# Two convolutions on TensorE: weights first, side taps without the padding columns, and a new order of the lead-in work

## The chip, the cores and the metric

One core of one Trainium2 chip runs the kernel. The metric is the device time in microseconds (us) of one execution; smaller is better.

## The reference, cut to what matters

```python
# x: (16, 32, 128, 128) fp32; w3: (32, 32, 3, 3); w5: (32, 32, 5, 5)
w3 = w3 * mask            # mask per (input channel, tap): mean |w3| over outputs > threshold
x = x + conv3x3(groupnorm(x, 16 groups), w3, zero padding 1)
x = x + conv5x5(groupnorm(x, 16 groups), w5, zero padding 2) + bias
# the 5x5 one is written as an FFT product in the reference
```

## The kernel before, in words

Each image is cut into two halves of 64 rows, so there are HALVES = 32 half images and the main loop has STEPS = 35 steps. Step s does the 3x3 convolution of half s (for s below 32) and the 5x5 convolution of half s - 3 (LAG = 3). A half is held as four bands of 16 rows; band i lies on partitions 32i to 32i+31 with the 32 channels in them, plus halo rows. Rows are 128 pixels wide and lie at a pitch of 132, with two zero columns at each side.

To keep fp32 accuracy with fp16 matmuls, image and weights are each split into a high and a low fp16 part (x3_hi, x3_lo, x5_hi, x5_lo; s3_hi, s3_lo, s5_hi, s5_lo), and three products are summed in PSUM: high with high, image high with weight low, image low with weight high. A matmul contracts the 32 channels of one band and streams 4 rows of 128 pixels, 512 columns. `pairs` (L868) puts two vertical taps side by side, on tiles of 32x64, so that 8 matmuls of different bands and column halves run at the same time in the array; `singles` (L886) does the outer vertical taps, on 32x32 tiles, 16 at a time. I call these 8 or 16 simultaneous matmuls a group. Per step the 3x3 part has 18 pair groups and 9 single groups, the 5x5 part 60 and 15. In both functions the loop over the horizontal taps dx is outermost.

TensorE's order in a full step: `pairs3_high` (3x3, high image), `pairs3_low` (needs x3_lo), `pairs5_high` (needs x5_hi and a free PSUM half), `singles3`, `singles5`, `pairs5_low`, which ends the 5x5 sum (`b5_whole`). 

The other engines, in hand-written order, tied by semaphores:

- VectorE (DVE): `setup3` (mask and split of w3, starts at L592 when w3 and the threshold are in), `stats_in` (L615, mean and variance of the loaded bands, 4 instructions for a half), `combine` or `group_stats` and `scale_of` (the group norm's factors), `normalize3` (L691), `low3` (L719, makes x3_lo), `low5` (L727), `take_conv3` (L739, adds x to the 3x3 sum, making `mid`; it then frees the 3x3 banks with `bank3_go`), `stats_out` (L747), `aggregate` (L625, which tells ScalarE by `mv_ready`), and for the last steps `take_late` and `add_late` (L757, L764).
- ScalarE (ACT): `take_conv5` (L468, four instructions that empty the 5x5 banks into conv_out), then `x5_hi_go`, which lets `pairs5_high` start; `gather_stats` (a DMA that spreads every partition's statistics to all partitions), `take_root` (L385), `normalize5` (L438), `high3` (L392), `high5` (L431), and last in a step with an exchange `spread_stats`, which waits for `mv_ready` and sends the statistics to DRAM. ACT does these strictly in this order, so the `take_conv5` of the next step stands behind `spread_stats`.
- GpSimd (POOL): the zero rows, then the DMAs that move `mid` of half 1 into bands (L363), then `add_out` (L369), which adds conv_out to `mid`.
- SyncE (SP): the other DMAs: `load_bands`, `load_own` (x again, in the layout of the output), `move_mid`, `store_out`.

Statistics of x for a pair of halves are exchanged in steps 2 and 4 and then in odd steps (`exchanged`); the 5x5 statistics in odd steps from 3. From half LATE = 29 on, ACT takes only two of the four 5x5 banks and DVE the other two.

Of the kernel before, what the change touches and what calls it, by code (L numbers as in the profile page):

```python
# [30 lines left out]
C = 32  # L31
Q = 4
# [17 lines left out]
def two_blocks(nc, x, w3_dram, thr_dram, w5_dram, bias_dram, mix_dram, out):  # L50
# [7 lines left out]
    with ExitStack() as ctx:  # L58
# [66 lines left out]
        w5_bounded = sem("w5_bounded")  # L125
        w5_hi_made = sem("w5_hi_made")
# [72 lines left out]
        LATE = HALVES - LAG  # L199
# [47 lines left out]
        def _(sp):  # L247
# [35 lines left out]

            load_bands(0)
            load_bands(1)
            load_bands(2)
            for q in range(Q):
                sp.dma_start(w5[quad(q), :, :], w5_dram.rearrange("i a b o -> i (a b) o")).then_inc(w_loaded, 16)
                sp.dma_start(bias[quad(q), :], bias_dram.rearrange("(o a) -> o a", a=1)).then_inc(w_loaded, 16)
# [51 lines left out]
        def _(pool):  # L341
# [18 lines left out]
            for i in range(Q):  # L360
                for j in range(Q):
                    to, rows = piece(1, i, j)
                    pool.dma_start(to, rows).then_inc(mid1_moved, 16)  # L363

# [6 lines left out]
            for k in range(LAST):  # L371
                for b in range(BANKS if k < LATE else HALF_BANKS):
                    add_out(k, b)
                if k == LATE:
                    pool.wait_ge(norm2, HALVES)
                    m = mid[:, LAST % MID_SLOTS, :, :]
                    nc.gpsimd.tensor_scalar(m, m, bias[:, 0:1], None, ALU.add).then_inc(bias_added, 1)

        @block.scalar
        def _(act):  # L380
# [39 lines left out]
            def high_w5():  # L420

                act.wait_ge(w5_bounded, 1)
                nc.scalar.activation(s5_hi[:, :, :], w5[:, :, :], ACT.Identity,
                                     bias=zeros[:, 0:1], scale=wfac[:, 1:2]).then_inc(w5_hi_made, 1)
# [38 lines left out]
            def take_conv5(k, b):  # L463

                act.wait_ge(b5_whole, k + 1)
# [22 lines left out]
            act.dma_start(mix_in[:, :], mix_dram).then_inc(mix_loaded, 16)  # L488
            by_scalar = 1
# [5 lines left out]
            for s in range(STEPS + 1):  # L495
# [5 lines left out]
                if HALVES < s <= LAST + LAG:  # L501
                    act.wait_ge(late_out, s - HALVES)
# [38 lines left out]
        def _(dve):  # L541
# [207 lines left out]
            def take_late(k):  # L749

                dve.wait_ge(b5_whole, k + 1)
                if k == LATE:
                    dve.wait_ge(out_added, BANKS * LATE)
                else:
                    dve.wait_ge(late_added, k - LATE)
# [4 lines left out]
            def add_late(k):  # L760
# [8 lines left out]
            set_apart("x", 0)  # L769
            dve.drain().then_inc(bank3_go, 1)  # L770
# [15 lines left out]
            dve.wait_ge(w_loaded, 16 * 2 * Q)  # L786
            largest(w5, 1)
# [26 lines left out]
            for s in range(LAG + 1, STEPS):  # L814
                gathered = exchanged(s - 1)
                if s > HALVES:
                    take_late(s - 1 - LAG)
                low5(s - LAG)
                if s > HALVES:
                    add_late(s - 1 - LAG)  # L820
# [11 lines left out]
                if s % 2:  # L832
# [14 lines left out]
                if has3(s + 1):  # L847
                    low3(s + 1)
# [9 lines left out]
        def _(pe):  # L858
            def pairs(w, src, k, bank, start=False, every=None):

                for dx in range(k):
                    x0 = 2 - k // 2 + dx
                    for dy in range(1, k):
                        at = dx * k + k - 1 - dy
                        for i in range(Q):
                            for J in range(2):
                                top = 2 * J + dy
                                ins = nc.tensor.matmul(  # L868
                                    psum[2 * C * J:2 * C * (J + 1), bank + i, :].rearrange("p (a w) -> p a w", a=A),
                                    w[quad(i), at:at + 2, :].rearrange("p t o -> p (t o)"),  # L870
                                    src[quad(i), top:top + A * (A - 1) + 1:A, x0:x0 + W],
                                    start=start and dx == 0 and dy == 1, stop=True, skip_group_check=True,
# [5 lines left out]
            def singles(w, src, k, bank, start=False):  # L878

                for dx in range(k):  # L880
                    x0 = 2 - k // 2 + dx
                    for i in range(Q):
                        for j in range(Q):
# [3 lines left out]
                                psum[quad(j), bank + i, :].rearrange("p (a w) -> p a w", a=A), w[quad(i), at, :],  # L887
                                src[quad(i), j + dy:j + dy + A * (A - 1) + 1:A, x0:x0 + W],
                                start=start and dx == 0, stop=True, skip_group_check=True, tile_position=(i * C, j * C))
# [130 lines left out]
```

## Time and profile before

| | |
|---|---|
| median of 3 runs | 823.47 us (822.88 to 823.75) |
| the profiled execution | 823.28 us |
| its span, first to last instruction | 821.5 us |
| PE busy / DVE / ACT / POOL | 756.0 / 608.8 / 333.9 / 265.3 us |
| matmuls | 32292 |
| mean granted TensorE clock | 0.980 |
| DMA | 150.76 MB, mean 184 GB/s |

The span is 1.8 us shorter than the profiled execution, which is 0.2 us below the median of the runs. Engines overlap; PE is busy 92% of the span, so the question at each place is whether PE waits there, and for whom. L with a number is a line of the kernel; an engine's name with q (ACTq, DVEq) is its instruction queue.

### The profile page before, as it was taken

Reading aid. Unit: us, or ns where it says so; the run is one execution under the profiler, and the core shown is the slowest. Engines: PE = TensorE matmul, PEld = TensorE weight load, DVE = VectorE, ACT = ScalarE, POOL = GpSimd, SP = SyncE. Lnnn points to the kernel's source line nnn. Section 1 sums busy time; section 2 is a strip of 40 time slices with the busy share of each in tenths; the row PEclk is TensorE's granted clock in tenths of the full one; section 3 lists DMA queues with packets and bytes.
Section 4 is the critical chain, followed back from the end, with each engine's and each line's share of the span. In section 5 each row is a group of like instructions: output and inputs, shape, how many; then the busy total and the mean of one; then the engine's idle time right before and its main releaser. Section 6 shows DMA issues by size and latency. Waiting matters only on the chain.

```text
span 821.5 us, 67804 instructions
## 1 busy us (share of the span) xinstructions
PE 756.0 (92%) x32292; PEld 528.7 (64%) x32292; DVE 608.8 (74%) x970; ACT 333.9 (41%) x289; POOL 265.3 (32%) x161
## 2 busy tenths in 40 slices
PE   0585898899999999999999999999999999998996
PEld 0252484568767667767766766776776676676664
DVE  2888757797878969787879878787878786663341
ACT  0252314344443636344443536353443436362420
POOL 1021034044434332233434343222434343322360
PEclk9997898999999999999999999999999999999998
DMA  9879399989997989899897979898997956673424
GB/s 203 158 143 224 75 217 227 230 205 220 195 222 171 220 195 221 196 218 212 202 217 168 219 183 227 196 225 198 215 219 181 220 116 161 137 167 86 99 51 102
DMA packets 234400, 150.76 MB, mean 184 GB/s; under 512 B 18752, under 2 KB 227712, under 8 KB 230272
## 3 DMA queue, kind: packets, MB, share of 16 engines
q1 hardware_dynamic: 227200, 143.93, 80.8%
q10 hardware_dynamic: 6464, 5.24, 2.7%
q0 software_dynamic: 704, 1.25, 0.6%
q8 instruction: 10, 0.16, 0.1%
q14 instruction: 22, 0.18, 0.1%
HBM read 75.86 MB, written 33.59 MB: 133 GB/s over the span
## 4 chain that ended last, share of the span: by engine, by line
PE 82%; DVE 8%; DMA 4%; issue 2%; DVEq 1%; ACT 1%; ACTq 1%
PE psum L868 63%; PE psum L886 20%; DMA every_mv<-mv_scratch 2%; DVE bn_in L615 2%; DMA thr<-L_conv_threshold_dram 1%; DVE x_lo L719 1%; DVE bn_out L747 1%; DMA mv_scratch<-mv 1%; DVE mid L739 1%; DVEq L742 1%; ACT conv_out L468 0%; ACTq L506 0%; ACTq L486 0%; DVE x_bands L691 0%; ACT x_hi L399 0%
## 5 line engine op out<-in xcount | busy, mean ns | idle before, releaser
L369 POOL TENSOR_TENSOR mid<-mid,conv_out 128x512 f32<-128x512 f32 x120 | 246.0, 2082 | 484.0 <-ACT conv_out L468 484.0
L868 PE MATMUL psum<-x_hi,s_hi 32*64 32x512 f16 x6656 | 201.3, 384 | 18.2 <-ACTq L506 6.2
L868 PE MATMUL psum<-x_lo,s_hi 32*64 32x512 f16 x6656 | 200.1, 383 | 5.9 <-DVE x_lo L719 5.9
L868 PE MATMUL psum<-x_hi,s_lo 32*64 32x512 f16 x6656 | 199.7, 381 | 0.0
L868 PEld LDWEIGHTS psum<-x_hi,s_hi 32*64 32x64 f16 x6656 | 122.0, 105 | 85.9 <-issue 11.2
L868 PEld LDWEIGHTS psum<-x_hi,s_lo 32*64 32x64 f16 x6656 | 133.6, 105 | 53.6 <-issue 4.3
L868 PEld LDWEIGHTS psum<-x_lo,s_hi 32*64 32x64 f16 x6656 | 108.9, 104 | 83.8 <-issue 11.6
L739 DVE SCALAR_TENSOR_TENSOR mid<-psum,unscale,x_own 128x1024 f32<-128x1024 f32 x64 | 79.1, 1278 | 90.5 <-PE psum L886 90.4
L468 ACT ACTIVATE conv_out<-psum,bias,unscale 128x512 f32<-128x512 f32 x120 | 83.7, 777 | 69.7 <-PE psum L868 60.7
L392 ACT ACTIVATE x_hi<-x_bands 128x2304 f16<-128x2304 f32 x31 | 65.6, 2117 | 106.2 <-PE psum L886 106.2
L727 DVE TENSOR_TENSOR x_lo<-mid_bands,x_hi 128x2560 f16<-128x2560 f32 x32 | 93.8, 2932 | 6.9 <-PE psum L868 6.8
L431 ACT ACTIVATE x_hi<-mid_bands 128x2560 f16<-128x2560 f32 x31 | 72.5, 2339 | 50.8 <-PE psum L886 48.8
L385 ACT ACTIVATE root<-gvar 128x1 f32<-128x1 f32 x32 | 6.5, 203 | 207.7 <-DVE gvar L668 175.2
L438 ACT ACTIVATE mid_bands<-mid_bands,nbias,gscale 128x2560 f32<-128x2560 f32 x31 | 78.2, 2524 | 16.0 <-DVE nbias L682 13.6
L747 DVE BATCH_NORM_STATS2 bn_out<-mid 128x6 f32<-128x512 f32 x128 | 79.1, 680 | 4.1
L719 DVE TENSOR_TENSOR x_lo<-x_bands,x_hi 128x2304 f16<-128x2304 f32 x32 | 80.7, 2522 | 0.6 <-ACT x_hi L392 0.2
L615 DVE BATCH_NORM_STATS2 bn_in<-x_bands 128x6 f32<-128x512 f32 x128 | 76.7, 663 | 2.6 <-DMA x_bands<-x_dram 2.6
L886 PE MATMUL psum<-x_hi,s_hi 32*32 32x512 f16 x4096 | 74.3, 378 | 1.8 <-issue 1.7
L886 PE MATMUL psum<-x_hi,s_lo 32*32 32x512 f16 x4096 | 73.4, 376 | 0.0
L691 DVE TENSOR_SCALAR x_bands<-x_bands,gmean,gscale 128x2304 f32<-128x2304 f32 x29 | 67.8, 2339 | 0.5 <-ACT x_hi L403 0.4
L886 PE MATMUL psum<-x_lo,s_hi 32*32 32x512 f16 x4096 | 66.2, 377 | 1.4 <-issue 1.4
L886 PEld LDWEIGHTS psum<-x_hi,s_hi 32*32 32x32 f16 x4096 | 53.6, 88 | 19.7 <-issue 15.7
(91 smaller groups left out, 338.3 us busy)
## 6 DMA issues: line engine op xcount, KB each, us to landing
x_own<-x_dram SPq DMA_DIRECT2D x128, 256.0 KB, 5.0
mid_bands<-mid SPq DMA_DIRECT2D x372, 80.0 KB, 3.4
out_dram<-mid SPq DMA_DIRECT2D x116, 256.0 KB, 5.3
x_bands<-x_dram SPq DMA_DIRECT2D x96, 288.0 KB, 6.1
x_bands<-x_dram SPq DMA_DIRECT2D x32, 272.0 KB, 6.9
mid_bands<-mid SPq DMA_DIRECT2D x124, 64.0 KB, 2.9
every_mv<-mv_scratch ACTq DMA_DIRECT2D x17, 256.0 KB, 4.1
out_dram<-mid SPq DMA_DIRECT2D x20, 128.0 KB, 2.4
```

The costliest lines, as they stand in the source:

```text
L369: nc.gpsimd.tensor_tensor(m, m, conv_out[:, b, :], ALU.add).then_inc(out_added, 1)
L431: nc.scalar.activation(x5_hi[:, :, 2:2 + W], mid_bands[:, k % MB_SLOTS, :, :], ACT.Copy).then_inc(hi5_done, 1)
L438: nc.scalar.activation(v, v, ACT.Identity, bias=nbias[:, at], scale=gscale[:, at]).then_inc(act_scaled, 1)
L468: nc.scalar.activation(conv_out[:, b, :], psum[:, X5_BANK + b, :], ACT.Identity, bias=bias[:, 0:1], scale=unscale[:, 1:2]).then_inc(conv5_ ...
L615: nc.vector.bn_stats(bn_in[:, h // 2 % 2, h % 2, b, :], rows.rearrange("p a w -> p (a w)")).then_inc(bn_x, 1)
L691: nc.vector.tensor_scalar(v, v, gmean[:, 0:1], gscale[:, 0:1], ALU.subtract, ALU.mult).then_inc(scaled, 1)
L719: nc.vector.tensor_tensor(x3_lo[:, :, 2:2 + W], x_bands[:, h % XB_SLOTS, :, :], x3_hi[:, :, 2:2 + W], ALU.subtract).then_inc(x3_lo_go, 1)
L727: nc.vector.tensor_tensor(x5_lo[:, :, 2:2 + W], mid_bands[:, k % MB_SLOTS, :, :], x5_hi[:, :, 2:2 + W], ALU.subtract).then_inc(x5_lo_go, 1)
L739: nc.vector.scalar_tensor_tensor(mid[:, h % MID_SLOTS, at, :], psum[:, X3_BANK + at.start:X3_BANK + at.stop, :], unscale[:, 0:1], x_own[:, ...
L747: nc.vector.bn_stats(bn_out[:, h % 2, b, :], mid[:, h % MID_SLOTS, b, :]).then_inc(bn_mid, 1)
L868: ins = nc.tensor.matmul(psum[2 * C * J:2 * C * (J + 1), bank + i, :].rearrange("p (a w) -> p a w", a=A), w[quad(i), at:at + 2, :].rearran ...
L886: ins = nc.tensor.matmul(psum[quad(j), bank + i, :].rearrange("p (a w) -> p a w", a=A), w[quad(i), at, :], src[quad(i), j + dy:j + dy + A ...
```

## The change

Four things are changed.

1. Loads and weights. w3 is loaded first, half of it by SP ahead of the first bands and half by ACT; w5 is loaded before the bands of half 2; bias goes to ACT's queue, on a semaphore of its own. `largest(w5)` is done in the start by DVE, before `bank3_go`; POOL scales w5 and makes s5_lo; ACT's `high_w5` moves from step 1 to step 2 and waits for POOL's scaling.
2. LATE is 28 in place of 29, so one more half has its banks shared by ACT and DVE.
3. DVE's order. In step 4 (LAG + 1) `low3(5)` comes before the `stats_in` of halves 6 and 7. In step 5 (the only step where `just_now` holds) `take_conv3(5)` and `low3(6)` come before the `stats_in` of halves 8 and 9, and `stats_out(5)` after them.
4. Matmuls. The taps go in the order center, then outward; a tap at distance d from the center reads and writes 128 - d columns of each of its 4 rows (508 or 504 in place of 512), so the output in PSUM is 4 runs of 127 or 126 with gaps.

```diff
-        LATE = HALVES - LAG
+        LATE = HALVES - LAG - 1
...
+            for q in range(Q // 2):
+                sp.dma_start(w3[quad(q), :, :], ...).then_inc(w3_loaded, 16)
             load_bands(0)
             load_bands(1)
-            load_bands(2)
             for q in range(Q):
                 sp.dma_start(w5[quad(q), :, :], ...).then_inc(w_loaded, 16)
-                sp.dma_start(bias[quad(q), :], ...).then_inc(w_loaded, 16)
+            load_bands(2)
             load_bands(3)
...
                     pool.dma_start(to, rows).then_inc(mid1_moved, 16)
+            pool.wait_ge(w5_bounded, 1)
+            nc.gpsimd.tensor_scalar(w5[:, :, :], w5[:, :, :], wfac[:, 1:2], None, ALU.mult).then_inc(w5_scaled, 1)
+            pool.wait_ge(w5_hi_made, 1)
+            nc.gpsimd.tensor_tensor(s5_lo[:, :, :], w5[:, :, :], s5_hi[:, :, :], ALU.subtract).then_inc(w5_split, 1)
...
             def high_w5():
-                act.wait_ge(w5_bounded, 1)
-                nc.scalar.activation(s5_hi[:, :, :], w5[:, :, :], ACT.Identity,
-                                     bias=zeros[:, 0:1], scale=wfac[:, 1:2]).then_inc(w5_hi_made, 1)
+                act.wait_ge(w5_scaled, 1)
+                nc.scalar.activation(s5_hi[:, :, :], w5[:, :, :], ACT.Copy).then_inc(w5_hi_made, 1)
...
-            for q in range(Q):
+            for q in range(Q // 2, Q):
                 act.dma_start(w3[quad(q), :, :], ...).then_inc(w3_loaded, 16)
             act.dma_start(thr[:, :], ...).then_inc(w3_loaded, 16)
             act.dma_start(mix_in[:, :], mix_dram).then_inc(mix_loaded, 16)
+            for q in range(Q):
+                act.dma_start(bias[quad(q), :], ...).then_inc(bias_loaded, 16)
...
                     normalize3(3)
-                    high_w5()
                 elif s == 2:
                     high3(3)
+                    high_w5()
                     take_root(("mid", 0))
...
             stats_in(1, range(BANKS))
             set_apart("x", 0)
+            dve.wait_ge(w_loaded, 16 * Q)
+            largest(w5, 1)
             dve.drain().then_inc(bank3_go, 1)
...
             low3(2)
-            dve.wait_ge(w_loaded, 16 * 2 * Q)
-            largest(w5, 1)
             power_of_two(1)
...
             low3(LAG)
-            dve.wait_ge(w5_hi_made, 1)
-            nc.vector.scalar_tensor_tensor(s5_lo[:, :, :], w5[:, :, :], wfac[:, 1:2], s5_hi[:, :, :],
-                                           ALU.mult, ALU.subtract).then_inc(w5_split, 1)
...
-                if s % 2:
+                if s % 2 and not just_now:
                     for h in (s + 3, s + 4):
                         if has3(h):
                             stats_in(h, range(BANKS))
                 if has3(s):
                     take_conv3(s)
+                if just_now:
+                    low3(s + 1)
+                    for h in (s + 3, s + 4):
+                        stats_in(h, range(BANKS))
+                if has3(s):
                     stats_out(s)
                 if s == LAG + 1:
+                    low3(s + 1)
                     for h in (2 * LAG, 2 * LAG + 1):
                         stats_in(h, range(BANKS))
                     aggregate("x", LAG, mv_ready)
...
-                if has3(s + 1):
+                if has3(s + 1) and s != LAG + 1 and not just_now:
                     low3(s + 1)
...
+            def columns(k):
+                for dx in sorted(range(k), key=lambda d: abs(d - k // 2)):
+                    x0 = 2 - k // 2 + dx
+                    yield dx, x0, max(0, 2 - x0), min(W, W + 2 - x0)
...
-                for dx in range(k):
-                    x0 = 2 - k // 2 + dx
+                for dx, x0, c0, c1 in columns(k):
...
-                                    psum[...].rearrange("p (a w) -> p a w", a=A),
+                                    psum[...].rearrange("p (a w) -> p a w", a=A)[:, :, c0:c1],
...
-                                    src[quad(i), top:top + A * (A - 1) + 1:A, x0:x0 + W],
-                                    start=start and dx == 0 and dy == 1, stop=True, skip_group_check=True,
+                                    src[quad(i), top:top + A * (A - 1) + 1:A, x0 + c0:x0 + c1],
+                                    start=start and dx == k // 2 and dy == 1, stop=True, skip_group_check=True,
```

`singles` is changed in the same way. The conditions on `s > HALVES` around `take_late`, `add_late` and `late_out` follow LATE.

## Rows read from the trace of the kernel before

**Rows 1.** The page: busy time, and the groups of instructions with their mean

```profile
PE 756.0 (92%) x32292; PEld 528.7 (64%) x32292; DVE 608.8 (74%) x970; ACT 333.9 (41%) x289; POOL 265.3 (32%) x161
...
L719 DVE TENSOR_TENSOR x_lo<-x_bands,x_hi 128x2304 f16<-128x2304 f32 x32 | 80.7, 2522 | 0.6 <-ACT x_hi L392 0.2
```

**Rows 2.** The chain that ended last, in order of time: start, length, what

```profile
3.83 11.01 DMA thr<-L_conv_threshold_dram
...
22.52 4.77 DVE bn_in L615 x8
...
132.43 7.69 DMA mv_scratch<-mv
140.14 8.00 DMA every_mv<-mv_scratch
```

**Rows 3.** Windows: stretch, length, busy of PE, PEld, DVE, ACT, POOL, clock, DMA

```profile
208.70:231.50 22.80, 22.76 (x1008) 17.65 (x1000) 19.14 (x38) 10.49 (x10) 8.27 (x4) 1.00 0.93 209
```

**Rows 4.** Timeline of PE in one step: start, length, instruction, count

```profile
737.65 4.61 PE L868 MATMUL psum<-x_hi,s_hi 32*64 32x512 f16 x160
...
742.02 4.63 PE L868 MATMUL psum<-x_hi,s_lo 32*64 32x512 f16 x160
...
749.65 1.37 PE L886 MATMUL psum<-x_hi,s_hi 32*32 32x512 f16 x80
...
750.75 1.37 PE L886 MATMUL psum<-x_hi,s_lo 32*32 32x512 f16 x80
```

**Rows 5.** Timeline, the warming matmuls of L936, alone on PE

```profile
28.65 6.10 PE L936 MATMUL psum<-warm 128*128 128x512 f16 x14
...
51.67 1.90 PE L936 MATMUL psum<-warm 128*128 128x512 f16 x8
```

**Rows 6.** L868 at 737.64 to 738.51 (dx 0), then 738.51 to 739.39 (dx 1): min/median/max ns

```profile
L868 PE MATMUL psum<-x_hi,s_hi x32: 372/374/377, 737.6 to 738.4; 32*64 32x512 f16 x32
...
L868 PE MATMUL psum<-x_hi,s_hi x42: 372/377/381, 738.1 to 739.2; 32*64 32x512 f16 x42
```

**Rows 7.** The start: timeline of DVE, and issues at 0.7 to 1.2, 2.1 and 5.2 with us to landing

```profile
14.94 0.46 DVE L592 TENSOR_REDUCE score<-w 128x9 f32<-128x288 f32 x1 [13.13 <-DMA thr<-L_conv_threshold_dram]
...
w<-L_conv_weight_dram ACTq DMA_DIRECT2D x2, 36.0 KB, 5.4
...
w<-L_conv_weight_dram ACTq DMA_DIRECT2D x1, 36.0 KB, 7.8
...
x_bands<-x_dram SPq DMA_DIRECT2D x2, 272.0 KB, 11.0
```

**Rows 8.** Timeline around the weights of the 5x5 part, and POOL's bias instruction

```profile
55.71 9.21 POOL L363 DMA_DIRECT2D mid_bands<-mid  x16 [50.73 <-DVE mid L739]
...
60.44 1.05 ACT L423 ACTIVATE s_hi<-w,zeros,wfac 128x800 f16<-128x800 f32 x1 [2.53 <-DVEq L789]
...
67.46 0.20 ACT L385 ACTIVATE root<-gvar 128x1 f32<-128x1 f32 x1 [3.95 <-DVE gvar L653]
...
782.64 6.41 POOL L377 TENSOR_SCALAR mid<-mid,bias 128x2048 f32<-128x2048 f32 x1
```

**Rows 9.** Timeline of steps 4 to 6, with the waits that matter

```profile
132.86 2.79 ACT L468 ACTIVATE conv_out<-psum,bias,unscale 128x512 f32<-128x512 f32 x4 [3.02 <-DVE mv L625]
...
134.86 2.79 PE L868 MATMUL psum<-x_lo,s_hi 32*64 32x512 f16 x48 [3.64 <-DVE x_lo L719]
...
137.43 5.99 PE L868 MATMUL psum<-x_hi,s_hi 32*64 32x512 f16 x160
...
163.87 2.79 ACT L468 ACTIVATE conv_out<-psum,bias,unscale 128x512 f32<-128x512 f32 x4 [5.98 <-DVE mv L625]
...
167.22 4.59 PE L868 MATMUL psum<-x_hi,s_hi 32*64 32x512 f16 x160
```

**Rows 10.** Timeline of PE at the start of steps 32 and 33

```profile
759.61 4.61 PE L868 MATMUL psum<-x_hi,s_hi 32*64 32x512 f16 x160 [2.96 <-ACTq L506]
...
778.25 4.61 PE L868 MATMUL psum<-x_hi,s_hi 32*64 32x512 f16 x160 [1.61 <-ACTq L506]
```

More of the change, by code:

```diff
@@ L125, in two_blocks @@
         w5_bounded = sem("w5_bounded")
+        bias_loaded = sem("bias_loaded")
+        w5_scaled = sem("w5_scaled")
         w5_hi_made = sem("w5_hi_made")
@@ L282, in move_edges @@
                                      ).then_inc(mid_bands_in[2 * n % MB_SLOTS], 16)
+            for q in range(Q // 2):
+                sp.dma_start(w3[quad(q), :, :], w3_dram.rearrange("i a b o -> i (a b) o")).then_inc(w3_loaded, 16)
             load_bands(0)
             load_bands(1)
-            load_bands(2)
             for q in range(Q):
                 sp.dma_start(w5[quad(q), :, :], w5_dram.rearrange("i a b o -> i (a b) o")).then_inc(w_loaded, 16)
-                sp.dma_start(bias[quad(q), :], bias_dram.rearrange("(o a) -> o a", a=1)).then_inc(w_loaded, 16)
+            load_bands(2)
             load_bands(3)
@@ L373, in _ @@
                     add_out(k, b)
-                if k == LATE:
+                if k == LATE + 1:
+                    pool.wait_ge(bias_loaded, 16 * Q)
                     pool.wait_ge(norm2, HALVES)
@@ L463, in take_conv5 @@
             def take_conv5(k, b):
+                if k == 0 and b == 0:
+                    act.wait_ge(bias_loaded, 16 * Q)
                 act.wait_ge(b5_whole, k + 1)
@@ L488, in _ @@
             act.dma_start(mix_in[:, :], mix_dram).then_inc(mix_loaded, 16)
+            for q in range(Q):
+                act.dma_start(bias[quad(q), :], bias_dram.rearrange("(o a) -> o a", a=1)).then_inc(bias_loaded, 16)
             by_scalar = 1
@@ L500, in _ @@
                         take_conv5(k, b)
-                if HALVES < s <= LAST + LAG:
-                    act.wait_ge(late_out, s - HALVES)
+                if LATE + LAG < s <= LAST + LAG:
+                    act.wait_ge(late_out, s - LATE - LAG)
                 if s == LAG:
@@ L752, in take_late @@
                 if k == LATE:
+                    dve.wait_ge(bias_loaded, 16 * Q)
                     dve.wait_ge(out_added, BANKS * LATE)
@@ L815, in _ @@
                 gathered = exchanged(s - 1)
-                if s > HALVES:
+                if s > LATE + LAG:
                     take_late(s - 1 - LAG)
                 low5(s - LAG)
-                if s > HALVES:
+                if s > LATE + LAG:
                     add_late(s - 1 - LAG)
@@ L868, in pairs @@
                                 ins = nc.tensor.matmul(
-                                    psum[2 * C * J:2 * C * (J + 1), bank + i, :].rearrange("p (a w) -> p a w", a=A),
+                                    psum[2 * C * J:2 * C * (J + 1), bank + i, :].rearrange("p (a w) -> p a w", a=A)[:, :, c0:c1],
                                     w[quad(i), at:at + 2, :].rearrange("p t o -> p (t o)"),
-                                    src[quad(i), top:top + A * (A - 1) + 1:A, x0:x0 + W],
-                                    start=start and dx == 0 and dy == 1, stop=True, skip_group_check=True,
+                                    src[quad(i), top:top + A * (A - 1) + 1:A, x0 + c0:x0 + c1],
+                                    start=start and dx == k // 2 and dy == 1, stop=True, skip_group_check=True,
                                     tile_position=(i * C, 2 * C * J))
@@ L876, in pairs, with singles @@
                 return ins
-            def singles(w, src, k, bank, start=False):
-                for dx in range(k):
-                    x0 = 2 - k // 2 + dx
+            def singles(w, src, k, bank):
+                for dx, x0, c0, c1 in columns(k):
                     for i in range(Q):
@@ L886, in singles @@
                             ins = nc.tensor.matmul(
-                                psum[quad(j), bank + i, :].rearrange("p (a w) -> p a w", a=A), w[quad(i), at, :],
-                                src[quad(i), j + dy:j + dy + A * (A - 1) + 1:A, x0:x0 + W],
-                                start=start and dx == 0, stop=True, skip_group_check=True, tile_position=(i * C, j * C))
+                                psum[quad(j), bank + i, :].rearrange("p (a w) -> p a w", a=A)[:, :, c0:c1], w[quad(i), at, :],
+                                src[quad(i), j + dy:j + dy + A * (A - 1) + 1:A, x0 + c0:x0 + c1],
+                                start=False, stop=True, skip_group_check=True, tile_position=(i * C, j * C))
                 return ins
```

## The prediction

> **What bounds the kernel now.** I read the page first: PE is busy 756 of 821.5 us [rows 1]. The chain of waits then shows where it is not the bound: the start, which waits for a DMA of the threshold, and the lead-in up to 167 us, where DVE and two exchanges through DRAM hold the chain [rows 2]. The windows show that from 186 us on every full step takes 22.80 us with PE busy all the time at the full clock (one such step stands in [rows 3]); this repeats up to 756 us. So TensorE's own pace sets the middle, DVE and DMA the lead-in, and short waits for ACT the last steps [rows 10]. The DMA engines are at 0.93 in the step shown, which leaves room for a step shorter by one per cent.
>
> Next, what sets PE's pace. The 160 pair matmuls of one product take 742.02 - 737.65 = 4.37 us, for 20 groups of 8, so 219 ns a group; 80 singles take 750.75 - 749.65 = 1.10 us, 220 ns for a group of 16 [rows 4]. A warming matmul alone, with the same 512 columns, goes at (1.90 - 0.39)/7 = 0.216 us at the full clock and at 6.10/14 = 0.43 us at the lower one (2.4 and 1.2 GHz) [rows 5]. A group of 8 or of 16 thus costs what one stream of 512 columns costs, 213 ns at 2.4 GHz, and some 6 ns. Columns are what is paid for, not instructions. Of the 6 ns a part comes from where the read starts: the matmuls of tap 0 have a median of 374 ns, those of tap 1, which start at an odd column, 377 [rows 6].
>
> **The change part by part.** *Columns.* A side tap at distance 1 streams 4 columns fewer, 1.67 ns, and one at distance 2 streams 8 fewer, 3.33 ns. Per step the 3x3 part has 27 groups, 18 of them at distance 1: 30 ns. The 5x5 part has 75, of which 30 at each distance: 150 ns. Together 0.18 us of 22.80, 0.8%. Where PE is the bound (5x5 of halves 2 to 31 and 3x3 of halves 6 to 31) that is 30 x 0.150 + 26 x 0.030 = 5.3 us, and about 0.2 more before that: **-5.5 us**. What the trace doesn't show is a matmul that writes runs with gaps: all of them write 512 columns in one piece. Bounds: on the side of a gain, the start column costs 3 ns at most [rows 6] and the new starts (2, 2, 2, 3, 4 in place of 0 to 4) could give that back at one tap in five, another 0.05 us a step or 1.5 us; on the other side, the nearest row of a slower stream is the lower clock, twice the time, taken up among the rivals. I take the column count.
>
> The Trainium skill ("PSUM — Partial Sum Buffer", specifications, and "Advanced Engine Details and Errata", PSUM Cachelines) speaks against this: PSUM has 8-byte lines, and an access pattern in which not every two consecutive elements are contiguous slows matmuls significantly. No run here shows it so far; by it the term would be a loss, which the first rival works out from rows.
>
> *Start.* DVE's first work waits 13.13 us for the threshold, which was issued at 3.83 and took 11.0 us, behind four loads of w3 on its queue and in competition with twelve loads of bands [rows 2, 7]. Now only two w3 loads are ahead of it on that queue, and it is issued at about 1.7. Late bound: the first two w3 loads took 5.4 us in the median (the second was in at about 7.1), and the threshold follows as long after them as it followed the last one before (3.83 + 11.01 = 14.8, less 2.1 + 7.8 = 9.9: 4.9 us), at 12.0: a gain of 2.9 us. Early bound: it takes 5.4 us like those loads and lands at 7.1: 7.8 us. From there on the bands of half 1 bind as well: they landed at 16.4 at the latest (issued at 5.2 to 5.7, 11.0 us) [rows 7] and come 0.9 us later now, and their statistics started at 24.9 [rows 2]. Since the bands no longer run ahead of the weights I take a value on the early side, a landing at 8.1: **-6.8 us**. All that follows in the start hangs on this: statistics, their mixing on PE, factors, first matmul. The added `largest` (0.98 us) covers most of the 0.77 us that DVE waited for that mixing: **+0.3**. The wait for w5 costs nothing: with w3 (0.15 MB), two halves (2.3) and itself (0.4) it has 2.9 MB to wait for, 14 us at the 209 GB/s of [rows 3] and some 2 to start, and DVE gets there at about 21. Nor do the own rows of half 0, 6.2 MB in all and in at about 32, hold up DVE's first take of a 3x3 sum.
>
> *w5 on POOL.* ACT's `high_w5` now stands behind POOL, whose 16 DMA issues run until 55.71 + 9.21 = 64.92 [rows 8], 9.2 us after the second half's `mid` whatever DVE does (times as before, the start's shift left out). Scaling 800 elements at 6.41/2048 = 3.1 ns each takes 2.5 us: 67.4. The copy takes ACT about 1.0 [rows 8], until 68.5. Queued behind it on ACT is `take_root` of the first 5x5 statistics, which ran at 67.46. Behind that are `scale_of`, `low3(3)` and `high5_first`, and PE waits for both. DVE itself loses two instructions of 1.0 us, but they are not late any more, the root is: **+1.1 us** (0.9 to 1.8 if POOL is slower while DVE runs). s5_lo is ready at about 71.8, before x5_hi at 72.9.
>
> *DVE's order in steps 4 and 5.* PE waited 3.64 us for x3_lo of half 5 [rows 9], and `low3(5)` comes first now. But ACT's take of the 5x5 banks waited for `mv_ready` (3.02 us) and so did the next one (5.98 us) [rows 9], since `spread_stats` stands ahead of it, and x5_hi_go behind. In step 4 `low3` (2.5 us [rows 1]) now stands ahead of the aggregate: mv_ready at 134.9 in place of 132.4 [rows 2], conv_out (2.79 us) until 138.3, and the 5x5 pairs start at 138.4 where they started at 137.43. PE only waits in another place. The exchange, two DMAs of 7.7 and 8.0 us [rows 2], starts 2.5 us later, and what hangs on it in step 5 too. There `low3(6)` again stands ahead of the aggregate, another 2.5 us. So mv_ready of step 5 comes 5 us later, and the 5x5 pairs, which started at 167.22 half a us after x5_hi_go, start **4.7 us** later; ahead of that PE has only the 3x3 pairs to do (4 us) and idles for some 8. Bounds: if the DMAs, which compete with bands and moves, land when they landed before, 2.3; no gain is possible here, since the chain between the aggregates only gets longer.
>
> *The clock.* After the idle stretch before 134.86 the clock was at the lower level, and 48 + 160 matmuls took 2.79 + 5.99 us where full speed takes 1.53 + 4.6 [rows 4, 9]: 2.6 lost. Before, PE came out of this place at 167 at full speed. Now it comes out of a longer idle stretch: **+2.4**, 0 to 3.
>
> *LATE.* In step 32 PE waited 2.96 us for ACT's four banks, in step 33, where DVE takes two, 1.61 [rows 10]. Step 32 now goes like 33: **-1.4**. DVE's added 3.6 us there have the 9 us of pairs [rows 4] as cover; without it they would come back in full.
>
> Sum: -6.8 + 0.3 + 1.1 + 4.7 + 2.4 - 1.4 - 5.5 = -5.2. The profiled execution took 823.28 (span 821.5 and 1.8 around it), which gives 818.1; the median of the runs is 0.2 above it: **818.3 us**, 0.6% faster.
>
> **The rivals.**
>
> *Runs of 127 are written slowly.* Suppose that writes go well only by pairs of neighbouring columns: an odd run then puts half of its rows out of step, and each pair there is written twice. Two of four rows at half pace, which is that of the lower clock [rows 5], add 2 x 127/2.4 = 106 ns to each group at distance 1. There are 48 of them a step, so 5.1 us, and the kernel would take about 823 + 30 x 5 = 970 us. It decides from little: 78 side groups a step share 5.2 + 5.5 = 10.7 us of advantage, 0.36 us a step, so 4.6 ns more per side group than I assume makes the kernel slower. For it: nothing in the trace shows a gapped write. Against it: odd starts and rows at a pitch of 132 on the reading side cost 3 ns a group, not 100 [rows 6]. Chance 0.15. This is what the rule of the Trainium skill's PSUM page, named above, would do here.
>
> *The columns save nothing.* A run of 127 or 126 costs what 128 cost, on either side. Then 818.3 + 5.5 = 823.8, no change. For it: the reading side already pays something that isn't columns. Chance 0.17.
>
> *The new order works as written.* The exchange isn't late, PE's waits for x3_lo go and the clock stays up. Then 4.7 + 2.4 become about 0: 811. Against it: the two waits of ACT for mv_ready. Chance 0.14.
>
> *The start gains its late bound only:* -2.9 for -6.8, 822.2. This is in my own case's range.
>
> My case, all terms in their bounds, has 0.52; its own range is 814 to 823. What is left, 0.02, is none of these.
>
> **How the numbers follow.** The range goes from the third rival to the top of the second with the late start, 811 to 827; it leaves out the 0.15 of slow writes and a little at both ends. About 0.2% (1.7 us) is what can be told from no change. Faster: 0.44 of my case's 0.52, all 0.14 of the third rival, 0.05 of the second one's 0.17: 0.63. Within 0.2%: 0.04 of my case and 0.06 of the second: 0.10. Slower: the rest, 0.27.
>
> **What would show it.** Steps of 22.62 us in place of 22.80 in the windows, with groups at distance 2 some 3 ns shorter; a step of over 23 means slow writes. DVE's first instruction at about 8 us. ACT's root of the 5x5 statistics waiting for POOL. In step 4, PE's wait moved from x3_lo to ACT; in step 5, conv_out waiting for mv_ready longer than 5.98 us, and PE waiting about 8 us for ACTq. PE's wait at step 32 about 1.6. The prediction is wrong if gapped writes have a price, or if the exchange's DMAs take up or add several us, as their times move with the traffic.

## The result, and the profile after

The changed kernel takes 817.43 us (median of 5 runs, 815.5 to 818.38), the kernel before in the same session 823.47 (5 runs, 822.79 to 825.56). The ratio is 0.9916, 95% interval 0.9901 to 0.993: 0.8% faster (these two medians alone are 6.0 us apart, 0.7%; the ratio gives 6.9 us). The median is 0.9 us below the forecast of 818.3. The profiled execution has a span of 816.6 us, 4.9 less than before.

The total came out; several terms did not. First the page's busy time and the head of the chain of waits (start, length, what), which answer [rows 1] and [rows 2]:

```profile
PE 751.8 (92%) x32292; PEld 528.8 (65%) x32292; DVE 612.0 (75%) x971; ACT 332.4 (41%) x287; POOL 262.3 (32%) x161
```

```profile
1.66 7.66 DMA thr<-L_conv_threshold_dram
...
51.23 8.46 POOL mid_bands L366 x15
...
68.14 7.04 PE psum L888 x139
...
102.89 11.18 DMA every_mv<-mv_scratch
...
133.52 11.10 PE psum L888 x190
...
163.31 11.60 PE psum L888 x280
```

The threshold now lands 7.66 us after its issue, where it took 11.01, and POOL's moves are on the chain, where they were not before. Next the windows of exactly 22 steps, from the first 3x3 matmul of one step to that of the 22nd after it, before (first fence) and after (second); columns as in [rows 3]:

```profile
232.03:733.67 501.64, 501.64 (x22184) 357.27 (x22176) 402.91 (x606) 227.25 (x197) 179.12 (x88) 1.00 0.89 196
```

```profile
230.14:730.35 500.21, 500.21 (x22185) 359.41 (x22177) 405.18 (x606) 227.25 (x197) 179.06 (x88) 1.00 0.89 197
```

PE never waits in either. A step went from 501.64/22 = 22.80 to 500.21/22 = 22.74, not to 22.62. One product of a step shows it without any sum: the timeline after, which answers [rows 4] and, in its last two rows, [rows 10].

```profile
734.31 4.60 PE L888 MATMUL psum<-x_hi,s_hi 32*64 32x512 f16 x160
738.69 4.61 PE L888 MATMUL psum<-x_hi,s_lo 32*64 32x512 f16 x160
...
754.91 4.59 PE L888 MATMUL psum<-x_hi,s_hi 32*64 32x512 f16 x160 [1.62 <-ACTq L517]
...
773.47 4.59 PE L888 MATMUL psum<-x_hi,s_hi 32*64 32x512 f16 x160 [1.61 <-ACTq L517]
```

The 20 groups took 4.38 us from start to start, and 4.37 before, although 16 of them now stream 4 or 8 columns fewer. The wait at step 32 is 1.62 where it was 2.96.

The start and the detour over POOL (timeline, answering [rows 7] and [rows 8]):

```profile
9.42 0.46 DVE L603 TENSOR_REDUCE score<-w 128x9 f32<-128x288 f32 x1 [7.62 <-DMA thr<-L_conv_threshold_dram]
...
50.44 9.26 POOL L366 DMA_DIRECT2D mid_bands<-mid  x16 [45.45 <-DVE mid L750]
...
59.84 2.29 POOL L368 TENSOR_SCALAR w<-w,wfac 128x800 f32<-128x800 f32 x1
...
62.16 0.87 ACT L431 ACTIVATE s_hi<-w 128x800 f16<-128x800 f32 x1 [4.21 <-POOL w L368]
...
63.12 1.70 POOL L370 TENSOR_TENSOR s_lo<-w,s_hi 128x800 f16<-128x800 f32 x1 [0.99 <-ACT s_hi L431]
...
63.36 1.48 DVE L687 TENSOR_TENSOR newton<-gvar,rinv 128x1 f32<-128x1 f32 x1
...
77.17 1.70 PE L888 MATMUL psum<-x_hi,s_hi 32*64 32x504 f16 x51 [1.99 <-issue]
```

DVE starts 5.5 us earlier. `newton`, one element per partition, usually takes 0.16 us and took 1.48 here, beside POOL's subtraction. The last row's wait is marked "issue": PE waited for nothing that the profile shows. It stands in the first passage of PE through the 5x5 part and in no later step; it was 5.24 us before and is 1.99 now. That it is a wait for code is a guess, which no run here tests.

Steps 4 to 6, answering [rows 9]:

```profile
130.65 2.79 ACT L477 ACTIVATE conv_out<-psum,bias,unscale 128x512 f32<-128x512 f32 x4 [5.74 <-DVE mv L636]
...
133.52 6.76 PE L888 MATMUL psum<-x_hi,s_hi 32*64 32x512 f16 x160 [6.75 <-ACTq L517]
...
135.50 0.33 ACTq L490 DMA_DIRECT2D every_mv<-mv_scratch  x1
...
141.36 0.40 DVE L671 SCALAR_TENSOR_TENSOR product<-every_mv,mix_in 128x128 f32<-128x128 f32 x1 [8.53 <-DMA every_mv<-mv_scratch]
...
160.44 2.79 ACT L477 ACTIVATE conv_out<-psum,bias,unscale 128x512 f32<-128x512 f32 x4 [7.92 <-DVE mv L636]
...
163.31 7.21 PE L888 MATMUL psum<-x_hi,s_hi 32*64 32x512 f16 x160 [4.74 <-ACTq L517]
```

PE's wait has moved from x3_lo to ACT, as the prediction said, and is 6.75 us long; the next is 4.74. Both times PE then runs at its lower clock for a part of the product: 160 matmuls take 6.76 and 7.21 us, where they take 4.6 at the full one.

### The profile page after: what moved, and what is told of

Same layout as the page of the kernel before. It is cut to its first block, busy times and chain, and to the rows that moved or that the text cites. A ratio compares the mean times of both kernels' runs of the same rounds, so it can differ in the third digit from the quotient of the medians.

```text
span 816.6 us, 67808 instructions
## 1 busy us (share of the span) xinstructions
PE 751.8 (92%) x32292; PEld 528.8 (65%) x32292; DVE 612.0 (75%) x971; ACT 332.4 (41%) x287; POOL 262.3 (32%) x161
## 4 chain that ended last, share of the span: by engine, by line
PE 84%; DVE 7%; DMA 2%; issue 2%; POOL 1%; ACT 1%; ACTq 1%; DVEq 1%; POOLq 0%
PE psum L888 64%; PE psum L905 20%; DVE bn_in L626 2%; DVE x_lo L730 2%; DMA every_mv<-mv_scratch 1%; POOL mid_bands L366 1%; DMA thr<-L_conv_threshold_dram 1%; ACTq L517 1%; DVE mid L750 1%; ACT conv_out L477 1%; DVE bn_out L758 0%; DVEq L753 0%; ACT mid_bands L445 0%; ACTq L401 0%; ACT x_hi L407 0%
## 5 line engine op out<-in xcount | busy, mean ns | idle before, releaser
L376 POOL TENSOR_TENSOR mid<-mid,conv_out 128x512 f32<-128x512 f32 x118 | 238.9, 2054 | 486.4 <-ACT conv_out L477 486.4
L888 PE MATMUL psum<-x_hi,s_hi 32*64 32x508 f16 (+2 forms) x6656 | 203.3, 387 | 22.7 <-ACTq L517 16.3
L888 PE MATMUL psum<-x_lo,s_hi 32*64 32x508 f16 (+2 forms) x6656 | 197.9, 379 | 6.1 <-DVE x_lo L730 5.4
L888 PE MATMUL psum<-x_hi,s_lo 32*64 32x508 f16 (+2 forms) x6656 | 196.7, 376 | 0.9 <-issue 0.9
L888 PEld LDWEIGHTS psum<-x_hi,s_hi 32*64 32x64 f16 x6656 | 123.7, 106 | 91.7 <-ACTq L517 18.7
L905 PE MATMUL psum<-x_hi,s_hi 32*32 32x508 f16 (+2 forms) x4096 | 74.0, 377 | 1.8 <-issue 1.7
L905 PE MATMUL psum<-x_hi,s_lo 32*32 32x508 f16 (+2 forms) x4096 | 73.4, 376 | 0.0
L905 PE MATMUL psum<-x_lo,s_hi 32*32 32x508 f16 (+2 forms) x4096 | 65.8, 376 | 1.7 <-issue 1.7
```

The source lines that it names most:

```text
L376: nc.gpsimd.tensor_tensor(m, m, conv_out[:, b, :], ALU.add).then_inc(out_added, 1)
L888: ins = nc.tensor.matmul(psum[2 * C * J:2 * C * (J + 1), bank + i, :].rearrange("p (a w) -> p a w", a=A)[:, :, c0:c1], w[quad(i), at:at + ...
L905: ins = nc.tensor.matmul(psum[quad(j), bank + i, :].rearrange("p (a w) -> p a w", a=A)[:, :, c0:c1], w[quad(i), at, :], src[quad(i), j + d ...
```

## The experiments

Times are given as ratios to the kernel before on the same chip, so that they compare across sessions. Lone profiled executions of kernels with the same order of loads differ by up to 4.9 us at the first wait (DVE starts at 5.9 us in one and at 10.8 in another), so a stage is judged inside one trace.

### The columns

**The new columns alone.** The kernel before, with only TensorE's part of the change:

```
+ for dx in sorted(range(k), key=lambda d: abs(d - k // 2)):
+     yield dx, x0, max(0, 2 - x0), min(W, W + 2 - x0)
```

> The kernel before with item 4 of the change alone (center tap first, side taps of 508 or 504 columns). By my prediction, a group costs its columns: 0.18 us less a step, 22.62 us, and 5.5 us in all, 818.0. By what the trace after suggests, only rows that lie within 16 units of 8 columns of the source tile get cheaper: steps of about 22.74, 1.5 to 2 us in all, 821.7. If gapped writes had a price, the kernel would be slower than before.

Measured: 0.9983 (0.9971 to 0.9996), 1.4 us. The other 5.5 us of the change's gain are elsewhere.

**The whole change, at full width** (order of the taps kept):

```
- yield dx, x0, max(0, 2 - x0), min(W, W + 2 - x0)
+ yield dx, x0, 0, W
```

> The changed kernel with all taps at 512 columns again, center first. By my prediction it loses 5.5 us: 823. By the second theory (a row of the source costs by the 16-byte pieces it touches once it touches 17 of them) it loses 1.5 to 2 us: 819.2, steps of 22.80.

Measured: 0.9926 (0.9912 to 0.994), beside the change's 0.9916: no difference that can be told. In the profile the step is shorter without the missing columns. The window of 22 steps:

```profile
228.26:727.37 499.11, 499.11 (x22186) 352.39 (x22178) 400.43 (x606) 227.18 (x197) 178.53 (x88) 1.00 0.89 198
```

That is 22.69 us a step, against 22.74 with them and 22.80 before. So leaving columns out costs 0.05 us a step, and what little the step gained comes with the center tap first, the only other thing that is changed on TensorE in these steps.

**Only the taps at distance 2 are cut** (126 columns), those at distance 1 stay at 128:

```
+ yield (dx, x0, max(0, 2 - x0), min(W, W + 2 - x0)) if abs(dx - k // 2) == 2 else (dx, x0, 0, W)
```

> The changed kernel, with 512 columns again for taps at distance 1 and 504 for those at distance 2. By the price of columns it loses a third of the term, 48 groups x 1.67 ns = 0.08 us a step, 2.4 us: 819.9. By the second theory taps at distance 1 never gained anything: no difference from the changed kernel, 817.4 within 0.5.

Measured: 0.9922 (0.9904 to 0.994), a step of 22.75. Again nothing. The groups by form, from 320 to 640 us, of the changed kernel (x_hi,s_hi pairs with 4 x 127, 4 x 126 and 4 x 128 columns; the last number but one is the mean ns of one):

```profile
L888 PE MATMUL psum<-x_hi,s_hi 32*64 32x508 f16 x1352 | 43.1, 378 | 0.0
...
L888 PE MATMUL psum<-x_hi,s_hi 32*64 32x504 f16 x896 | 27.0, 373 | 0.0
L888 PE MATMUL psum<-x_hi,s_hi 32*64 32x512 f16 x688 | 24.7, 378 | 0.0
```

and of the full-width kernel:

```profile
L888 PE MATMUL psum<-x_hi,s_hi 32*64 32x512 f16 x2936 | 85.7, 375 | 0.0
```

A run of 127 is paid like a run of 128; 126 is some 5 ns shorter, and the full-length ones around it a little longer. The distance from the start of one group of pairs to that of the next, worked out from the starts of the single matmuls in the trace, gives the same with less blur (medians over 24 steps), and it sorts by something else than columns. A row of 128 fp16 columns is 256 bytes. If it begins on a 16-byte boundary it touches 16 pieces of 16 bytes, and its groups start 215 ns apart; if not, it touches 17, and they are 218 to 223.5 apart, at any of the other starts. The kernel before shows both inside one tap: a row of the tile is 264 bytes, 16.5 pieces, so for tap 0 only every other input row begins on a boundary, and in the product of [rows 4] its four groups take 220, 215, 221 and 215 ns. With rows 132 columns apart and the picture at column 2, no row of 127 or 128 of the changed kernel begins on a boundary, and only half of the groups of 126 touch as few as 16 (those: 212 ns; the other half, with 17 pieces: 218 to 220).

**Rows on a boundary.** The changed kernel with the padding columns gone from memory, which is possible because no tap streams them any more:

```
- PITCH = W + 4
+ PITCH = W
- x0 = 2 - k // 2 + dx
- yield dx, x0, max(0, 2 - x0), min(W, W + 2 - x0)
+ x0 = -(k // 2) + dx
+ yield dx, x0, max(0, -x0), min(W, W - x0)
- nc.scalar.activation(x3_hi[:, :, 2:2 + W], x_bands[:, h % XB_SLOTS, :, :], ACT.Copy)
+ nc.scalar.activation(x3_hi[:, :, 0:W], x_bands[:, h % XB_SLOTS, :, :], ACT.Copy)
```

x3_lo, x5_hi and x5_lo are written likewise, and the eight memsets of the padding are gone. Now every row that a tap streams touches 16 pieces: at -1 and -2 it begins at column 0; at +1 and +2 it begins at column 1 or 2, off a boundary, but ends with the row and so stays within its 16.

> The changed kernel with the fp16 image tiles at a pitch of 128 columns without padding columns (nothing reads them any more), so that every row starts at a 16-byte boundary and every tap touches at most 16 pieces of 16 bytes. By the price of columns alone nothing changes: 817.4 within 1. By the second theory all groups fall to columns/2.4 ns + 1.7: 215.0, 213.4 and 211.7 ns for 512, 508 and 504 columns, that is 24 x 215.0 + 48 x 213.4 + 30 x 211.7 = 21.75 us + 0.42 for the changes of tile shape = 22.17 us a step in place of 22.73, some 16 us in all: 801.

Measured: 0.9761 (0.9748 to 0.9774), 13 us faster than the change. The same views, three forms, then one product of the timeline, then the 22 steps:

```profile
L887 PE MATMUL psum<-x_hi,s_hi 32*64 32x508 f16 x1408 | 43.3, 375 | 0.0
...
L887 PE MATMUL psum<-x_hi,s_hi 32*64 32x504 f16 x960 | 28.2, 371 | 0.0
...
L887 PE MATMUL psum<-x_hi,s_hi 32*64 32x512 f16 x704 | 24.3, 374 | 0.0
```

```profile
721.28 4.48 PE L887 MATMUL psum<-x_hi,s_hi 32*64 32x512 f16 x160
725.58 4.48 PE L887 MATMUL psum<-x_hi,s_lo 32*64 32x512 f16 x160
```

```profile
227.09:717.40 490.31, 490.31 (x22186) 328.26 (x22177) 400.93 (x606) 227.11 (x197) 180.17 (x88) 1.00 0.92 201
```

Every form is 2 to 4 ns shorter, the product takes 4.30 us instead of 4.38, the step 22.29 instead of 22.74: 0.45 x 29 steps = 13 us, the whole gain. Expected were 22.17 us a step and 16 us in all. Most of what is missing are the 48 groups of 508: among aligned rows they still cost what 512 cost (groups 216 ns apart both, and 216 to 217 where the row begins at column 1, so the pieces count and not the start), while 504 cost 3.5 ns less, 8 columns at 2.4 GHz within the rounding. So the missing columns do count, but in twos, as far as 127 and 126 show it. Whether an odd run is rounded up where it is read (two fp16 columns) or where it is written (two fp32 columns) no run tells.

The Trainium skill ("Advanced Engine Details and Errata", SBUF Cachelines) says that SBUF is read in 16-byte lines and that a new line per access has a price. That fits the step from 16 to 17 pieces; that it shows even for neighbouring columns is this case's measurement.

**The pieces, or the pitch?** Full width again, rows 144 apart, picture at column 8: the center tap begins on a boundary, the side taps don't.

```
- PITCH = W + 4
+ PITCH = W + 16
- nc.scalar.activation(x3_hi[:, :, 2:2 + W], x_bands[:, h % XB_SLOTS, :, :], ACT.Copy)
+ nc.scalar.activation(x3_hi[:, :, 8:8 + W], x_bands[:, h % XB_SLOTS, :, :], ACT.Copy)
- yield dx, x0, max(0, 2 - x0), min(W, W + 2 - x0)
+ yield dx, x0, 0, W
```

> The changed kernel with every tap at its full 128 columns again, and with rows 144 apart and the picture at column 8, so that the center tap's rows start on a 16-byte boundary and those of the side taps do not. Theory A (what costs is the 17th 16-byte piece that a row of 128 columns touches when it does not start on a boundary): of the 3x3 taps one third gains over the full-width kernel with rows 132 apart, of the 5x5 taps one fifth, as there; a step of about 22.6 us, the time 816 to 818. Theory B (what the aligned kernel gained came from the pitch or from the zeroing that is gone, not from the pieces): a step of 22.3 us and 805 to 808. Theory C (the columns left out were the gain of the aligned kernel): a step of 22.69 and 818.3, as with full width at 132.

Measured: the step is 497.20/22 = 22.60 us, theory A's number:

```profile
230.96:728.16 497.20, 497.20 (x22185) 323.50 (x22177) 400.69 (x606) 227.07 (x197) 179.10 (x88) 1.00 0.89 198
```

The time, 0.987 (0.9843 to 0.9897), 813.9 us, is lower than A's 816 to 818, 4.6 us below the full-width kernel at 132 (0.9926). The shorter step explains 0.09 x 29 = 2.6 of them, and the other 2.0 lie within the two intervals. That the profiled spans are alike (814.1 and 813.8) is the luck of the start: DVE began at 10.78 us in this trace and at 5.99 in that one. The step decides for A, against the pitch itself and against the columns.

### The start

**The loads as before** (w3 wholly on ACT's queue, bands of half 2 ahead of w5, `largest` of w5 where it stood).

```
- for q in range(Q // 2):
-     sp.dma_start(w3[quad(q), :, :], w3_dram.rearrange("i a b o -> i (a b) o"))
- for q in range(Q // 2, Q):
+ for q in range(Q):
      act.dma_start(w3[quad(q), :, :], w3_dram.rearrange("i a b o -> i (a b) o"))
```

> The changed kernel with the loads in the old order (all of w3 on ACT's queue, bands of half 2 ahead of w5, largest of w5 late). The start term says it loses 5.5 us: PE's first 3x3 matmul at 34.7 in place of 29.1, 823. If the lead-in was held by something else, it loses less.

Measured: 0.9995 (0.9982 to 1.0008): the change's whole gain is gone, 6.5 us. DVE's first work waits 14.26 us for the threshold again (7.62 after), and the first 3x3 of half 3 starts at 67.38 in place of 59.95:

```profile
16.07 0.45 DVE L601 TENSOR_REDUCE score<-w 128x9 f32<-128x288 f32 x1 [14.26 <-DMA thr<-L_conv_threshold_dram]
```

### The weights of the 5x5 part

**Scaled on ACT and subtracted on DVE, as before:**

```
- nc.gpsimd.tensor_scalar(w5, w5, wfac[:, 1:2], None, ALU.mult)
- nc.gpsimd.tensor_tensor(s5_lo, w5, s5_hi, ALU.subtract)
+ nc.vector.scalar_tensor_tensor(s5_lo, w5, wfac[:, 1:2], s5_hi, ALU.mult, ALU.subtract)
```

> The changed kernel with the scaling and splitting of w5 on DVE and ACT as before, the rest (loads, the early largest) as changed. By my term the POOL detour costs 1.1 us; the trace after shows DVE's newton step L687 taking 1.48 us in place of 0.16 while POOL subtracts, so PE's x3_lo of half 3 should come 2 to 2.5 us earlier here, 66 in place of 68.1. The kernel gains up to that, 815.5, unless the exchange of half 3's statistics and its DMAs swallow it (then no difference).

Measured: 0.9903 (0.9879 to 0.9927), the same as the change. The x5 pairs of half 0 start at 65.90 instead of 70.70, and of these 4.8 us 1.1 are left when ACT's queue lets the 5x5 pairs of step 4 go (132.40 and 133.52):

```profile
74.12 2.59 PE L888 MATMUL psum<-x_hi,s_hi 32*64 32x504 f16 x51 [3.98 <-issue]
...
132.40 6.37 PE L888 MATMUL psum<-x_hi,s_hi 32*64 32x512 f16 x160 [6.59 <-ACTq L514]
```

The threshold was in 1.2 us earlier here, so 3.6 of the 4.8 are POOL's. Step 4 starts at 98.69 and 99.55, 0.9 us apart: PE gives 2.0 back at the "issue" wait (3.98 for 1.99), and the rest goes with a lower clock (granted 0.86 from 74.12 to step 4, and 1.00 in the same stretch of the change). So POOL's detour costs nothing that can be told: what PE reaches earlier, it waits for.

### VectorE's order in steps 4 and 5

**The old order in the changed kernel:**

```
- if s % 2 and not just_now:
+ if s % 2:
- if just_now:
-     low3(s + 1)
-     for h in (s + 3, s + 4):
-         stats_in(h, range(BANKS))
- if has3(s + 1) and s != LAG + 1 and not just_now:
+ if has3(s + 1):
```

> The changed kernel with DVE's order of the kernel before in steps 4 and 5 (low3 last, stats_in of halves 8 and 9 ahead of take_conv3). By my prediction the new order costs 4.7 us and 2.4 us of clock, so this is 5 to 7 us faster than the changed kernel: about 812, with the 5x5 pairs of half 3 starting at about 158 in place of 163.3. The rival, that the new order helps, has it 3 to 5 us slower, PE waiting for x3_lo and bank3_go again.

Measured: 0.9879 (0.9859 to 0.9898), 3 us faster than the change, with 5 to 7 expected. In the two traces step 4 and what follows, up to the start of the 22 steps, is 5 us shorter, so the old order is worth 3 to 5 us. The waits are those of before (3.02 and 5.98 in [rows 9]), and the clock stays up afterwards (1.53 us for 48 matmuls in the last row):

```profile
127.37 2.78 ACT L477 ACTIVATE conv_out<-psum,bias,unscale 128x512 f32<-128x512 f32 x4 [3.09 <-DVE mv L636]
...
157.48 2.78 ACT L477 ACTIVATE conv_out<-psum,bias,unscale 128x512 f32<-128x512 f32 x4 [5.99 <-DVE mv L636]
...
159.49 1.53 PE L883 MATMUL psum<-x_lo,s_hi 32*64 32x512 f16 x48 [2.75 <-DVE x_lo L730]
```

**The statistics ahead of the wait for the exchange,** in steps 4 and 5, `low3` ahead of the aggregate as in the change:

```
+ if s in (LAG + 1, LAG + 2):
+     for h in (2 * (s - 1), 2 * (s - 1) + 1): stats_in(h, range(BANKS))
  if gathered:
      dve.wait_ge(mv_in, 16 * exchange_number(s - 1))
```

> The changed kernel, with the stats_in of halves 6 and 7 in step 4 and of halves 8 and 9 in step 5 put ahead of DVE's wait for the exchange (8.7 and 8.5 us idle in the changed kernel), and the aggregate of x in step 4 right behind scale_of, so that mv_ready is no longer late for ACT. If PE's waits for x5_hi_go come from mv_ready behind stats_in and low3, as I hold, both waits (6.8 us and more) nearly vanish: the 5x5 pairs of half 3 start at about 152 in place of 163.3, the clock stays up there (another 2 to 3 us), and the kernel takes 803 to 807. If they come from the exchange's DMAs themselves, it gains less than 3 us.

Measured: 0.9862 (0.9842 to 0.9882), 4.4 us faster than the change, less than half of what I expected. Step 4 does what it should (PE waits 0.90 us for ACT, not 6.75). In step 5 the bands of half 8 aren't in, and DVE stands still for them:

```profile
139.53 2.48 DVE L626 BATCH_NORM_STATS2 bn_in<-x_bands 128x6 f32<-128x512 f32 x4 [7.05 <-DMA x_bands<-x_dram]
...
158.28 7.18 PE L888 MATMUL psum<-x_hi,s_hi 32*64 32x512 f16 x160 [4.76 <-ACTq L517]
```

**Aligned rows and the old order together:**

> The aligned kernel (805.0) with VectorE's order of steps 4 and 5 as before the change. If the two gains are independent: 805.0 less 2.6 to 3.1, 802 to 802.5. Rival: in the aligned kernel TensorE's shorter steps run ahead of VectorE's and the order decides nothing, 805.

Measured: 0.9714 (0.9681 to 0.9746), 800.84 us. The gains are independent within the interval (0.9761 less 0.0037 would be 0.9724).

**The same, with the statistics of halves 6 and 7 early, in step 4 alone:**

```
+ if s == LAG + 1:
+     for h in (2 * LAG, 2 * LAG + 1): stats_in(h, range(BANKS))
```

and its `aggregate` right after the factors.

> As the kernel with the old order and aligned rows, but with the statistics of halves 6 and 7 ahead of the wait for the exchange in step 4 (their bands are in by then), those of halves 8 and 9 left where they were. Theory: half 2's x5 pairs come 2 us earlier than with the old order alone, as where both were moved, and half 3's are not held up by the bands' transfer: 800 to 801. Rival: the exchange of step 5 starts as late as before, since VectorE's work is only put elsewhere, and the gain at half 2 is lost at half 3: 802.

Measured: 0.9686 (0.9657 to 0.9715), 798.81 us, the fastest kernel here; the intervals of this one and the last overlap. PE's wait at half 2 shrinks to 1.00 us. ACT waits for the statistics of step 5 for 5.99 us, as with the old order alone (6.00), but that wait begins earlier: counted from the start of step 4 (101.40 here, 99.94 there), ACT sends them off at 55.2 us instead of 58.1, and the 5x5 pairs of half 3 start at 59.0 instead of 61.8. The first theory holds and the rival doesn't: what is gained at half 2 is kept at half 3.

```profile
130.34 4.50 PE L883 MATMUL psum<-x_hi,s_hi 32*64 32x512 f16 x160 [1.00 <-ACTq L516]
...
157.06 2.79 ACT L476 ACTIVATE conv_out<-psum,bias,unscale 128x512 f32<-128x512 f32 x4 [5.99 <-DVE mv L635]
```

### The end

**LATE at 29 again:** `LATE = HALVES - LAG`.

> The changed kernel with LATE at 29 again, the one edit at the end undone. The prediction's term: 1.4 us slower than the changed kernel, 818.8 on the scale of its 817.4. Rival: the end's order hides it, 817.4.

Measured: 0.9944 (0.9922 to 0.9966). The interval touches the change's, but the profile has the prediction's row, 1.32 us longer than after:

```profile
755.42 4.59 PE L888 MATMUL psum<-x_hi,s_hi 32*64 32x512 f16 x160 [2.94 <-ACTq L517]
```

## Why the prediction was right, and where it was not

The sum was -5.2 us, the profiled executions differ by -4.9. By stages, each read as the time between the same instructions in both timelines, the terms are:

- *Start*, -6.8 and +0.3: the 3x3 of half 3 starts at 59.95 instead of 66.25, **-6.3**, and the loads' experiment gives 6.5. The size is right, but only 5.3 of it is the threshold's (the 3x3 of half 2 starts at 49.98 instead of 55.25): it landed at 9.3 and not at 8.1. The other 1.0 is `largest(w5)`, 0.98 us, which no longer stands between `low3(2)` and the statistics of half 1, and of which the prediction said that it was not late any more. Where the threshold lands is also chance: in the eleven traces with the new order of loads DVE starts at 5.9 to 10.8 us, 8.5 in the mean.
- *w5 on POOL*, +1.1: from there to the x5 pairs of half 0 the kernel loses 3.9 us (6.82 before, 10.75 after), then the "issue" wait is 3.25 shorter. Up to step 4 (105.47 and 99.55) it is **+0.4**. The path was as described, root behind POOL: DVE waits 1.62 us for it, where it usually waits 0.27. Missing in it were `newton`, 1.3 us longer beside POOL, the lower clock after PE's longer wait (0.9 us in the 48 matmuls that follow), and the "issue" wait that gives PE's lateness back. The Trainium skill ("SBUF — State Buffer", Who interferes with whom) names the first: a DVE instruction with two SBUF inputs contends with a GpSimd instruction that reads SBUF. The trace agrees, 1.48 for 0.16 us, and `newton` ends with POOL's subtraction (64.84 and 64.82).
- *DVE's order*, +4.7 (bound 2.3): to the x5 pairs of half 3, 61.75 us from step 4 before and 63.76 after, **+2.0**. mv_ready came late, and the waits moved as said. What failed was the size. The exchange was one of the numbers that I took as fixed, 7.69 + 8.00 us; issued later it took 5.3 + 5.9 (130.19 to 135.50 to 141.36), and that gave back most of the delay. That is the case which I had called the bound. It is not chance: in the eight traces in which this exchange is sent off 30 to 31 us after the start of step 4 it takes 11.2 to 13.1 us, in the six in which it goes at 24 to 28 it takes 14.9 to 17.0. What takes up the time no run shows.
- *The clock*, +2.4: 160 matmuls took 7.21 for 4.59 us. By the start of the 22 steps measured above **+2.0**. Right.
- *Columns*, -5.5: **-1.7** over all steps (-1.43 in those 22), and not even that comes from the columns, since full width has shorter steps. This is the step that failed: "A group of 8 or of 16 thus costs what one stream of 512 columns costs, 213 ns at 2.4 GHz, and some 6 ns. Columns are what is paid for, not instructions." The runs show that a run of 127 costs what 128 costs, and that 4 of the 6 ns (219 against 215) are the 17th piece of rows off the 16-byte boundary. I had that row in hand (tap 0 at 374 ns, the one at an odd column at 377), put it down to the odd column and used it only as a bound of 1.5 us; it was a lead to 13. Tap 0's own spread, 372 to 377, already held both kinds of row.
- *LATE*, -1.4: **-1.3**. Right.

Together -6.3 + 0.4 + 2.0 + 2.0 - 1.7 - 1.3 = -4.9. So the right total is luck, errors that cancel: the columns brought 3.8 us less than I took, the new order, POOL and the clock cost 3.8 less (4.4 for 8.2). Of the rivals, "the columns save nothing" is what happened on TensorE, and the time was still lower than its 823.8 because the order's price was too high. Slow writes of odd runs did not happen: 508 columns take 378 ns in the changed kernel, as 512 do there. The Trainium skill's rule ("PSUM — Partial Sum Buffer", specifications) would have made gapped runs slow. The runs here do not bear it out: runs of 127 with one column missing between them take 375 ns, contiguous 512 take 374 in the same kernel. At most the rounding up to 128, 4 columns or 1.7 ns a group, could be a price of writing.

What stays open: why the center tap first makes a step 0.1 us shorter at full width (with the new columns alone and with the whole change it is 22.75 and 22.74, so the rest of the change doesn't explain it), why cutting columns of rows off the boundary costs 0.05 again, on which side an odd run is rounded up, and what PE's "issue" wait is for.

## What to carry to other kernels

Before trimming the streamed columns of a matmul, look at where its rows begin: here cutting 1% of the columns gave nothing, and laying every row within 16-byte boundaries gave 13 us of 817. Cut in twos, and use the cut to get rid of the padding. An order of work that removes one wait can lengthen the next one: when the exchange of statistics hangs on an aggregate, put nothing that can follow it ahead of it, and put early only what has already been loaded.

## What the runs showed of the hardware

- Groups of 8 or 16 simultaneous matmuls with rows of 128 fp16 columns start 215 to 217 ns apart (medians) when each row touches 16 pieces of 16 bytes, and 217 to 224 when it touches 17. Within 16 pieces rows of 127 cost what rows of 128 cost (216 ns), rows of 126 are 3.5 ns cheaper; with 17 pieces rows of 126 take 218 to 220.
- Writes with gaps, 126 out of each 128 fp32 columns, cost nothing that can be measured (212 ns for 4 x 126, 215 for contiguous 512); 127 out of 128 cost at most the 1.7 ns of the four columns that they don't save.
- A DVE instruction on one element per partition took 1.48 us in place of 0.16 while POOL subtracted two tiles.
- PE's "issue" wait at its first 5x5 matmuls gives back part of a wait ahead of it. From the first of these matmuls to the end of that wait PE takes 8.2 to 9.0 us in the three traces in which it had waited 0 to 2.25 us for x3_lo before (the kernel before, the columns alone, w5 on DVE), and 6.4 to 6.8 in the eleven in which it had waited 2.84 to 5.37. A wait removed there comes back by some 2 us.
- The exchange of statistics in step 4, two small DMAs through DRAM, takes 11.2 to 13.1 us when it is sent off 30 to 31 us after the start of the step, and 14.9 to 17.0 at 24 to 28.
